# Mixing weights of two mixture stages: from a TensorE broadcast into PSUM to a load from DRAM broadcast over the partitions

## The reference

```python
# 8 experts of 176 hidden features, top 2, one shared expert; B, S, D = 2, 512, 256
scores = sigmoid(x @ gate_w.T)                      # [token, 8]
weight = where(in_top_2(scores), scores, 0)
weight = 2.5 * weight / (sum(weight) + 1e-20)
for e in range(8):
    y += weight[:, e] * ((silu(x @ w1[e]) * (x @ w3[e])) @ w2[e])
y += (silu(x @ sw1) * (x @ sw3)) @ sw2              # the shared expert, unweighted
```

## Time and profile before

| | us |
|---|---|
| median of 3 runs | 952.69 |
| lowest, highest | 952.52, 954.47 |
| the profiled execution | 954.21 |
| its span, first to last instruction | 952.1 |
| mean granted clock of TensorE | 0.929 |
| PE busy | 784.3 (82%) |
| DVE busy | 606.3 (64%) |
| ACT busy | 406.0 (43%) |

### The profile page before, as it was taken

How to read it: one execution, slowest core, us unless ns; L and a number is a source line. 1 busy time by engine, 2 the same in 40 slices (tenths; PEclk the granted TensorE clock), 3 DMA queues, 4 the chain that set the end, 5 groups by cost and what they waited for, 6 DMA issues and landing times.

```text
span 952.1 us, 11955 instructions
## 1 busy us (share of the span) xinstructions
PE 784.3 (82%) x3901; PEld 524.1 (55%) x3915; DVE 606.3 (64%) x895; ACT 406.0 (43%) x625; POOL 227.3 (24%) x162
## 2 busy tenths in 40 slices
PE   3999955756793664889998999997799998795997
PEld 3688821222371221338886777775446776453676
DVE  5545669999967999985556545457713655912444
ACT  3454465554445554543333324452174432072221
POOL 0000045675704676560957000000000000000000
PEclk9999985998997699899999999998799999798999
DMA  9100000000000000006000100033000042000000
GB/s 314 33 1 1 1 1 0 0 0 1 0 0 0 0 0 0 0 0 205 1 0 1 19 1 1 1 78 105 21 2 1 23 111 67 4 25 0 1 1 23
DMA packets 21238, 24.79 MB, mean 26 GB/s; under 512 B 2746, under 2 KB 18821, under 8 KB 21157
## 3 DMA queue, kind: packets, MB, share of 16 engines
q1 hardware_dynamic: 19942, 23.57, 8.6%
q10 hardware_dynamic: 1254, 0.66, 0.3%
HBM read 19.92 MB, written 4.29 MB: 25 GB/s over the span
## 4 chain that ended last, share of the span: by engine, by line
PE 61%; DVE 22%; issue 10%; ACT 3%; POOL 1%; DVEq 1%; DMA 1%; SPq 0%; POOLq 0%; ACTq 0%
PE PS L401 41%; DVE shared L1411 6%; DVE shared L1421 6%; PE PS L717 2%; PE PS L638 2%; PE PS L766 2%; ACT shared L1101 2%; PE PS L678 1%; POOL shared L1689 1%; PE PS L598 1%; PE PS L542 1%; DVE route L1480 1%; PE PS L411 1%; PE PS L752 1%; DMA shared<-in_L_ffn_W_dram 1%
## 5 line engine op out<-in xcount | busy, mean ns | idle before, releaser
L1689 POOL TENSOR_TENSOR shared<-shared,xn_tok 128x1024 f32<-128x1024 f32 x64 | 150.4, 2352 | 85.5 <-DVE shared L1421 70.1
L1238 DVE TENSOR_TENSOR gated<-gated,PS 128x512 f32<-128x512 f32 (+1 forms) x84 | 57.6, 686 | 169.5 <-ACT gated L872 169.0
L401 PE MATMUL PS<-xnT,work_r 128*128 128x512 f32 (+1 forms) x624 | 154.7, 398 | 0.0
L1421 DVE TENSOR_TENSOR_SCAN shared<-PS,shared 128x1024 f32<-128x1024 f32 x64 | 145.7, 2279 | 0.0
L401 PE MATMUL PS<-weights_r,work_r 128*128 128x256 f32 (+1 forms) x1008 | 140.7, 291 | 3.1 <-DVE work_r L1245 3.1
L872 ACT ACTIVATE gated<-PS 128x512 f32<-128x512 f32 (+1 forms) x84 | 50.1, 597 | 215.8 <-PE PS L401 205.9
L401 PE MATMUL PS<-xnT,weights_r 128*128 (+1 forms) x552 | 139.2, 404 | 1.6 <-DVE xnT L1221 1.6
L401 PEld LDWEIGHTS PS<-weights_r,work_r 128*128 128x128 f32 (+1 forms) x1008 | 127.3, 192 | 15.7 <-issue 10.1
L401 PEld LDWEIGHTS PS<-xnT,work_r 128*128 128x128 f32 (+1 forms) x624 | 112.2, 185 | 28.6 <-issue 1.3
L638 PE MATMUL PS<-shared,cf 128*128 128x512 f32 x256 | 127.0, 624 | 0.0
L401 PEld LDWEIGHTS PS<-xnT,weights_r 128*128 128x128 f32 x552 | 102.9, 191 | 24.7 <-issue 3.6
(11 more groups left out here) (178 smaller groups left out, 925.7 us busy)
## 6 DMA issues: line engine op xcount, KB each, us to landing
shared<-in_L_ffn_W_dram SPq DMA_DIRECT2D x3, 1024.0 KB, 12.2
scratch_k<-shared SPq DMA_DIRECT2D x12, 128.0 KB
scratch_q<-shared SPq DMA_DIRECT2D x12, 128.0 KB
shared<-scratch_k SPq DMA_DIRECT2D x8, 192.0 KB
shared<-scratch_q SPq DMA_DIRECT2D x8, 192.0 KB
mamba_w<-in_L_ffn_w_dram SPq DMA_DIRECT2D x2, 704.0 KB, 5.3
beside<-in_L_ffn_w_dram SPq DMA_DIRECT2D x2, 704.0 KB, 7.5
mamba_w<-in_L_ffn_w_dram SPq DMA_DIRECT2D x1, 1408.0 KB, 8.5
```

Of the source, the lines that this page charges most:

```text
L401: last = nc.tensor.matmul(o, lhs[l], rhs[r], start=(start and i == 0), stop=(stop and i == 2))
L1238: return nc.vector.tensor_tensor(g, g, bank(2 + slot)[0:rows, :], ALU.mult)
L1421: v.tensor_tensor_scan(hst[:, (u % 2) * 2 * T:(u % 2 + 1) * 2 * T], decay[u % 2], dbx[:, u * 2 * T:(u + 1) * 2 * T], 0.0, ALU.mult, ALU.add)\
L1689: nc.gpsimd.tensor_tensor(hc[:, u * 2 * T:(u + 1) * 2 * T].rearrange("p (c t) -> p c t", c=2), hst[:, (u % 2) * 2 * T:(u % 2 + 1) * 2 * T] ...
```

## The change

The mixing weight of each chunk is no longer made by PE. `route_weights` stops after the float weights. PE transposes these (float, 8 rows) and ACT copies them to the first 8 rows of `sigT`. SP writes these 8 x 512 values to DRAM (`scratch_w`), waits, and then loads for each chunk a tile of 128 x 512 float (256 KB), each partition reading its expert's row; where a chunk spans two experts, that is two DMAs. A stage has 11 chunks and 18 such DMAs. The tiles take turns in three slots in SBUF (`comb_slots`): a new tile, the place of a constant that is no longer needed, and `sigT`. DVE multiplies with the slot and waits on its semaphore `cb0`, `cb1` or `cb2`. The load of chunk `p` waits until chunk `p - 3` has been multiplied. The loads of MOE0 batch 1 and MOE1 batch 0 are put between the moves of the attention: up to chunk 10, the moves of `c` 0, chunks 11 and 12, the moves of `c` 1; and up to chunk 7, the moves of `c` 0, chunks 8 to 10, the moves of `c` 1, chunks 11 and 12.

```diff
         combT = sb("combT", T, BF16)
+        comb_spare = sb("comb_spare", T)
         ones_row = sb("ones_row", P)
...
         scratch_k = nc.dram_tensor("scratch_k", (DC, 3, HD, HH, T), BF16, kind="Internal").ap()
+        scratch_w = nc.dram_tensor("scratch_w", (2 * NB, NE, T), F32, kind="Internal").ap()
         scratch_m = nc.dram_tensor("scratch_m", (HALVES, 3 * HH * TC, P), BF16, kind="Internal").ap()
...
         minus_one = cols[:, 48:49]
+        comb_slots = (comb_spare[:, :], expert_b[:, 0:2 * T].bitcast(F32), sigT[:, :])
+        comb_rows = sigT[0:NE, :]
         c_A = cols[:, 64:128]
...
             S[st] = stage_sems(st, ("up", "silu", "prod", "high", "hid", "used", "score", "sig", "sigt",
-                                    "comb", "combt", "combT", "cb", "mixed"))
+                                    "comb", "combt", "combT", "cw", "cb0", "cb1", "cb2", "mixed"))
         S[MAMBA] = stage_sems(MAMBA, ("xp", "z", "ini", "tap", "xc", "zs", "dt", "dtT", "bc", "stack", "dl", "abs",
...
                                     "s2", "p", "v4", "av", "o4", "ot", "otok", "oT_up", "oT", "rc"))
+
+        def experts_of(m):
+
+            r = m * P
+            while r < (m + 1) * P:
+                end = min((r // EH + 1) * EH, (m + 1) * P)
+                yield r // EH, r - m * P, end - m * P
+                r = end
+
+        def comb_pieces(b, p):
+
+            return sum(len(list(experts_of(MOE_ORDER[i]))) for c in range(b + 1) for i in range(2, MM)
+                       if i % 3 == p % 3 and (c < b or i <= p))
...
                     .then_inc(s["score"], 1)
-
-                def broadcast_weight(p, m):
-
-                    pe.wait_ge(s["combT"], b + 1)
-                    pe.wait_ge(s["prod"], HEAD + b * MM + p)
-                    nc.tensor.matmul(bank(4), expert_b[0:3 * NE, m * P:(m + 1) * P], combT[0:3 * NE, :],
-                                     start=True, stop=True).then_inc(s["cb"], 1)
...
                         pe.wait_ge(s["comb"], b + 1)
-                        parts = route[:, COMB_AT:COMB_AT + TC * 3 * NE // 2].bitcast(BF16)
                         for tc in range(TC):
-                            last = nc.tensor.transpose(bank(7)[0:3 * NE, :].bitcast(BF16)[:, tc * P:(tc + 1) * P],
-                                                       parts[:, tc * 3 * NE:(tc + 1) * 3 * NE], ident_b[:, :])
+                            last = nc.tensor.transpose(bank(7)[0:NE, tc * P:(tc + 1) * P],
+                                                       route[:, (TC + tc) * NE:(TC + tc + 1) * NE], ident[:, :])
                         last.then_inc(s["combt"], 1)
-                    if 2 < p < MM:
-                        broadcast_weight(p, m)
                     if p >= 2:
...
                         self.down_chunk(s, b, MM, p - 2, LAST_ROWS if d == MM - 1 else P, (w2_hi, w2_lo), d * D)
-                    if p == 2:
-                        if early:
-                            pe.wait_ge(S[ATTN]["vtok"], 2 * DC)
-                        broadcast_weight(p, m)
                     if late:
...
                         act.wait_ge(s["combt"], b + 1)
-                        nc.scalar.activation(combT[0:3 * NE, :], bank(7)[0:3 * NE, :].bitcast(BF16)[:, 0:T],
-                                             ACT.Copy).then_inc(s["combT"], 1)
+                        nc.scalar.activation(comb_rows, bank(7)[0:NE, :], ACT.Copy).then_inc(s["combT"], 1)
                     if p == MM // 2 and (st, b) == (MOE0, 0):
...
                         dve.wait_ge(s["mixed"], b * RC + p - 1)
-                        dve.wait_ge(s["cb"], b * RC + p - 1)
+                        dve.wait_ge(s[f"cb{p % 3}"], 16 * comb_pieces(b, p))
                         g = gated[:, (p % 2) * T:(p % 2 + 1) * T]
-                        nc.vector.tensor_tensor(g, g, bank(4), ALU.mult).then_inc(s["prod"], 1)
+                        nc.vector.tensor_tensor(g, g, comb_slots[p % 3], ALU.mult).then_inc(s["prod"], 1)
                     self.low(s, b, MM, p - 1, rows(p - 1))
...
                 score, weight = route[:, 0:n], route[:, n:2 * n]
-                rank, rest = route[:, 2 * n:3 * n], route[:, 3 * n:4 * n]
+                rank = route[:, 2 * n:3 * n]
                 total = route[:, 4 * n:4 * n + TC]
...
                 self.link(v.tensor_scalar(total, total, 2.5, None, ALU.mult))
-                self.link(v.tensor_tensor(w3d, w3d, total.unsqueeze(2).broadcast_to([P, TC, NE]), ALU.mult))
-                parts = route[:, COMB_AT:COMB_AT + n * 3 // 2].bitcast(BF16)\
-                    .rearrange("p (t i e) -> p t i e", t=TC, i=3)
-                r3 = rest.rearrange("p (t e) -> p t e", t=TC)
-                self.link(v.tensor_copy(parts[:, :, 0, :], w3d))
-                self.link(v.tensor_tensor(r3, w3d, parts[:, :, 0, :], ALU.subtract))
-                self.link(v.tensor_copy(parts[:, :, 1, :], r3))
-                self.link(v.tensor_tensor(r3, r3, parts[:, :, 1, :], ALU.subtract))
-                v.tensor_copy(parts[:, :, 2, :], r3).then_inc(s["comb"], 1)
+                v.tensor_tensor(w3d, w3d, total.unsqueeze(2).broadcast_to([P, TC, NE]), ALU.mult)\
+                    .then_inc(s["comb"], 1)
...
+            def weight_rows(st, b, first, end):
+
+                s = S[st]
+                rows = scratch_w[2 * (st == MOE1) + b]
+                if first == 2:
+                    sp.wait_ge(s["combT"], b + 1)
+                    sp.dma_start(rows, comb_rows).then_inc(s["cw"], 16)
+                    sp.wait_ge(s["cw"], 16 * (b + 1))
+                for p in range(first, end):
+                    if st == MOE0 and b == 0 and p == 2:
+                        sp.wait_ge(ld["const"], 32)
+                    sp.wait_ge(s["prod"], HEAD + b * MM + max(p - 2, 0))
+                    for e, r0, r1 in experts_of(MOE_ORDER[p]):
+                        sp.dma_start(comb_slots[p % 3][r0:r1, :], rows[e:e + 1, :].broadcast_to([r1 - r0, T]))\
+                            .then_inc(s[f"cb{p % 3}"], 16)
+
             load_x(0)
...
+            weight_rows(MOE0, 0, 2, MM)
             sp.wait_ge(moe_down, MM)
...
             def attention_moves(b):
-                s = S[ATTN]
+                s, st = S[ATTN], (MOE0, MOE1)[b]
+                pause = ((11, 13), (8, 11))[b]
                 sources = (("k", k_parts, scratch_k, k_stack), ("q", q_parts, scratch_q, q_stack))
                 for c in range(DC):
+                    weight_rows(st, 1 - b, (2, pause[0])[c], pause[c])
                     for quad in (2 * c, 2 * c + 1):
...
                                 row += slots * HD
+                weight_rows(st, 1 - b, pause[1], MM)
                 for half in range(HALVES):
...
             over_batches(sp, attention_moves, peeled=True)
+            weight_rows(MOE1, 1, 2, MM)
             for b in range(NB):
...
                 sp.dma_start(out[b].rearrange("(t p) d -> p t d", p=P),
```

## The result

The changed kernel takes 988.29 us (median of 3 runs, 988.02 to 990.34) against 952.69: a ratio of 1.037, 95% interval 1.035 to 1.039. The forecast was 972.6 with a range up to 984. It is slower, as said, but by 35.6 us and not by 19.9, and outside the range. The profiled execution has a span of 986.2 us against 952.1 and a mean granted clock of 0.913 against 0.929.

The account below looks back on a forecast made before the run. The mixture stages were taken as bound by PE, with the 0.32 us broadcast on its path. The four stages summed -4.0 + 8.2 + 17.5 - 1.8 = +19.9 us on the 952.69 median, so 972.6 us, range 956 to 984.

Parts of the forecast that it names:

- broadcasts: PE's weight broadcasts, 0.32 us per turn on the path; dropping turns 4 to 12 saves 2.9 us a stage.
- opening: Turns 2 and 3 of each mixture stage, awaiting the first weight load: -1.1, +1.1, +1.5 and +1.1 us by stage.
- SP's queue: Weight loads behind the attention's stack reads in MOE0 batch 1 and MOE1 batch 0, held 18.5 us; the deciding step.
- B: Mixture stage MOE0, batch 1: +8.2 us, with load 11 held behind stack reads.
- C: Mixture stage MOE1, batch 0: +17.5 us, with loads 8 and 11 held behind stack reads.
- A: Mixture stage MOE0, batch 0: -4.0 us, from -1.1 at its start and -2.9 for later turns.
- D: Mixture stage MOE1, batch 1: -1.8 us, from +1.1 at its start and -2.9 for later turns.
- (1): Loads in MOE0 batch 1 and MOE1 batch 0: only SP's order holds them; sum +2.3, 955.0 us; chance 0.07.
- (2): Loads behind stack reads: hold shorter than for writes, 13 us; sum +3.5, 956.2 us; chance 0.07.
- (3): Loads behind stack reads: not held at all; sum -9.0, 943.7 us; chance 0.07.
- (4): Weight loads slow in themselves, 128 rows read from one DRAM row; about +10 on top, 983 us; chance 0.09.
- (5): PE's weight products in the mixture stages: they were free and the change does nothing; chance none.

Follow-up runs that it names:

- e1_no_broadcast: Kernel before with the broadcasts of turns 4 to 12 left out and nothing loaded instead (wrong weights): 939.28 us, ratio 0.986.
- e4_act_queue: Changed kernel with the loads of chunks 5 to 12 issued by ACT, each behind its high part, SP keeping chunks 2 to 4: 955.96 us, ratio 1.0035.
- e2_distinct_rows: Changed kernel with each weight tile loaded from 128 different rows of input x, not one or two weight rows (wrong numbers): 982.87 us, ratio 1.031.
- e11_first_alone: As e4_act_queue, but SP issues the loads of chunks 3 and 4 only once that of chunk 2 has landed: 951.23 us, ratio 0.9994.
- e8_filler: As e4_act_queue, plus 20 products of constants on PE at turn 3 while it would stand: 946.14 us, ratio 0.993.
- e3_spread_q: Changed kernel with each multi-copy q read split into one read of 16 rows per copy, same bytes and place: 968.19 us, ratio 1.015.
- e9_double: Kernel before with each broadcast of turns 4 to 12 made twice: 959.85 us, ratio 1.008.
- e10_before_spread: Kernel before with the q reads split into loads of 16 rows, as in e3_spread_q: 952.97 us, ratio 1.0003.
- e7_hybrid_act: Changed kernel with chunks 2 to 4 by PE's broadcast again, loads of 5 to 7 by SP, 8 to 12 by ACT: 942.59 us, ratio 0.989.

## Why the prediction failed

The places were right, and so was the mechanism that decides. The size was wrong, and most of that is in the step that looked smallest. The change of each stage splits by three kernels: the nine broadcasts (e1_no_broadcast less before), the opening (e4_act_queue less e1_no_broadcast), and SP's queue (the change less e4_act_queue). In us, by profiled executions, with the forecast's own terms in brackets; its queue term is B's 8.2 and C's 17.5 less the -1.8 and -1.4 that it gave them without a hold:

| | broadcasts | opening | queue | stage |
|---|---|---|---|---|
| A | -2.4 (-2.9) | +1.9 (-1.1) | -0.5 (0) | -1.0 (-4.0) |
| B | -3.8 (-2.9) | +5.2 (+1.1) | +10.7 (+10.0) | +12.2 (+8.2) |
| C | -4.1 (-2.9) | +6.7 (+1.5) | +22.2 (+18.9) | +24.8 (+17.5) |
| D | -5.2 (-2.9) | +5.2 (+1.1) | 0.0 (0) | +0.1 (-1.8) |
| sum | -15.5 (-11.6) | +19.1 (+2.6) | +32.5 (+28.9) | +36.1 (+19.9) |

Outside the mixture stages the change gains 2.0 us, which makes 34.1 by the spans; the medians have 35.6. The medians of the same three kernels give -13.7, +16.7 and +32.3 over the whole program: the profiled execution of before lies 1.5 us above its median and that of e1_no_broadcast 1.5 below, so the first two sums are some 2 us larger here.

**The opening is the step that failed**: it misses by 16.5 us (14.1 by the medians), where the four stages together miss by 16.2; the other two columns nearly cancel (-3.9 and +3.6). Its first part is the load: "I take 2.4 us in all, between 1.8 and 3.3". It took 3.9 us in A and 4.2 to 4.3 in B, C and D from issue to DVE, outside the bounds. The rows it was taken from were a read of 24 KB and a store of 512 KB, and neither reads one row 128 times (about 1 us, e2_distinct_rows) or shares its way with loads issued behind it (0.8 us, e11_first_alone). The two were not taken out together. Its second part is the clock: 0.8 us were charged, in A alone, with the ground that the old kernel pays in A too. But with the longer load PE stands in every opening, and e8_filler shows 2.45 us a stage on average. In D the two terms are 4.15 - 2.4 + 2.45 = 4.2, and the miss is 4.1. In B one more microsecond is in the write to DRAM, 2.45 us instead of the 1.42 to 1.45 of the other three; there the terms make 5.4 and the miss is 4.1, so they don't simply add up in every stage.

**The queue** was right in kind, and e4_act_queue and e3_spread_q show it: loads behind the reads in SP's queue come late, those that ACT issues come in time, and those behind split reads come less late. "I take the write's 18.5 us for it" is 1.1 to 2.0 short: 19.6, 20.5, 19.9. That it came so near is partly luck. The 18.5 rests on writes behind the reads following each other at 0.62 us, and SP's rows of before show that they don't:

```profile
646.84 2.38 SPq L1631 DMA_DIRECT2D scratch_k<-shared  x1
649.26 0.67 SPq L1631 DMA_DIRECT2D scratch_q<-shared  x1
```

The last write was issued at 649.26 and not at 644.9 (five steps of 0.62 after 641.77), 6.6 us before it landed; when the first one landed no row says. And the hold isn't one thing: 6.6 to 8.1 us are SP's issue of the reads, 3.3 to 3.6 a load's own time (e3_spread_q), and the 8 to 10 that are left are what the reads do to a load behind them. C's other part comes out of the opening. Less the 9.4 us by which C begins later, load 7 was issued at 767.2 and not at 762.5, c=0's reads began at 774.7 and not at 769, and load 11 landed at 819.2 and not at 811.0.

**The broadcasts** were worth more than "0.32 us", 0.51 in a steady turn (e1_no_broadcast, e9_double), but in A, B and C nine of them gave less than 4.6, as not each turn is bound by PE. This error is to the good side.

The product from SBUF cost nothing (692 ns), as forecast, and the attentions weren't held.

**The rivals.** (1), only SP's order: refuted as the whole, since load 8 of C lands 13.8 us after its own issue, and since e3_spread_q gives 20 us and changes the reads' pieces alone, with more of SP's issues than before; but as a part it is real, some 12 us, the stands that e3_spread_q keeps. (2), a hold of 13 us: refuted for loads too by 19.6 to 20.5. The Trainium skill's rule on the engines of a DMA (same page and section) agrees in kind with e3_spread_q and e10_before_spread. The prediction's estimate of 13 us from that page's rate is too low: 19.6 to 20.5 were measured. (3), no hold: refuted. (4), slow loads: partly true, 5.4 us of its 10, without which (e2_distinct_rows, 982.9) the time would be inside the range. The forecast treated (1), (4) and the main case as exclusive, and gave (4) only a side's chance; its measured part was added to the main case and carried the time over the range's end. (5): refuted by e1_no_broadcast.

**Where the time is.** From the change at 988.3: 32.3 us are the place in SP's queue (e4_act_queue), some 20 of it the shape of the q reads and some 12 the place behind SP's issue of them (e3_spread_q); 9.8 are the clock after the openings (e8_filler); and the 6.9 from there to the 939.3 of e1_no_broadcast are what is left of the stand itself, net of the 8 broadcasts that e1_no_broadcast keeps. The 4.7 of e11_first_alone may lie in both of the last two; these runs don't split it.

## What to carry to other kernels

A load that replaces compute costs its place in the queue that carries it, so first list what stands ahead of it there, how long that takes to issue, and what shape its outermost dimension has; if anything is long, another engine's queue with an early issue, or a finer split, is worth more than a new order. The first of such loads is latency: keep the old way for the first chunks, where data is fresh, and load the rest, which made this change 9.9 us faster than the kernel before instead of 35.6 slower. And price a stand on PE with the slow products behind it; here it was 2.45 us on average for a stand of 4.

## What the runs showed of the hardware

- A load of 128 rows of 2 KB, all from one row in DRAM, took 3.9 to 4.3 us from issue to its user with loads behind it, 3.1 to 3.4 alone, and 2.7 to 3.2 from 128 different rows (of another tensor) with loads behind it.
- After PE stood some 4 us, its clock was at 0.50 for 5 us of work or more, at 2.45 us of the kernel's time on average; filled with products of constants (20 in 4.4 us) it stayed at 1.00.
- One bf16 product of 24 rows and 512 columns between float products costs 0.51 us, a second right behind it 0.21.
- Twelve stack reads held the loads behind them on the same queue for 19.6 to 20.5 us after the first was issued, with the DMA engines busy to 0.39 on average near the end. With the q reads split into pieces of 16 rows a load behind them took 3.3 to 3.6 us from its own issue and not 11.5 to 13.8. Loads that ACT issued from its own queue while such reads were out took up to 8.8 us (e4_act_queue) and 10.2 us (e7_hybrid_act); DVE waited for only one of them, 0.6 us, as they were issued two turns ahead.
